# Residual stored to the output early, feed-forward term added there by accumulating transfers from GpSimd

## The reference

```
x = x + attention(mix(x, cond_weights[token]))          # 32 heads, 8 key/value heads, causal, rotary
h = mix(x, cond2_weights[token])
q_in, s_in = quantize(h)        # s_in = max|h| / 448; h / s_in clipped to +-448, rounded to fp8 values
y = (q_in * s_in) @ (fp8(qweight) * w_scale).T + bias
q_out, s_out = quantize_no_rounding(y)                  # s_out = max|y| / 448; y / s_out clipped to +-448
out = x + q_out * s_out
```

## Time and profile before

| | us |
|---|---|
| median of 3 runs (lowest, highest) | 550.52 (549.91, 550.93) |
| the profiled execution | 550.2 |
| span in its profile, first to last instruction | 548.4 |
| TensorE busy | 519.4 (95% of the span) |
| VectorE busy | 353.9 (65%) |
| GpSimd busy | 232.1 (42%) |
| ScalarE busy | 212.3 (39%) |

### The profile page before, as it was taken

One profiled execution on the slowest core, in us unless ns is written; L12 is line 12 of the kernel. 1 busy time (PEld: TensorE's weight loads), 2 busy tenths in 40 slices (PEclk: granted clock), 3 DMA queues, 4 the chain that ended last, 5 costly groups with the idle time before them and its releaser, 6 DMA issues.

```text
span 548.4 us, 8842 instructions
## 1 busy us (share of the span) xinstructions
PE 519.4 (95%) x3244; PEld 414.9 (76%) x3244; DVE 353.9 (65%) x536; ACT 212.3 (39%) x372; POOL 232.1 (42%) x184
## 2 busy tenths in 40 slices
PE   4999999999999999999999999999999999999680
PEld 2987888888888888888888888888888888887420
DVE  5538255666676667666766676667566756675697
ACT  2514214342534263416341634253516251612524
POOL 4426422642664266426632673267326732610002
PEclk9899999999999999999999999999999999999875
DMA  7540500020012011201020202020202000000004
GB/s 250 178 154 0 173 2 1 1 97 1 16 64 96 0 32 44 96 0 52 24 96 0 73 3 96 0 76 2 93 0 76 5 1 0 2 1 0 2 0 153
DMA packets 18046, 26.88 MB, mean 49 GB/s; under 512 B 1995, under 2 KB 6219, under 8 KB 18028
## 3 DMA queue, kind: packets, MB, share of 16 engines
q1 hardware_dynamic: 18028, 26.63, 14.4%
HBM read 24.53 MB, written 2.10 MB: 49 GB/s over the span
## 4 chain that ended last, share of the span: by engine, by line
PE 90%; DVE 7%; issue 1%; DMA 1%; SPq 0%; ACT 0%; DVEq 0%
PE bank L526 27%; PE bank L527 26%; PE bank L528 26%; PE bank L590 3%; PE bank L577 3%; PE bank L518 1%; PE bank L645 1%; DVE f_max L911 1%; PE bank L506 1%; DVE xacc L964 1%; DVE v_all L959 1%; DMA wsc<-in_L_ffn_weight_scale 1%; DVE w L759 1%; DVE q_cos L212 1%; DVE v_all L906 0%
## 5 line engine op out<-in xcount | busy, mean ns | idle before, releaser
L780 DVE TENSOR_TENSOR q_cos<-bank,cst 128x512 f32<-128x512 f32 x80 | 55.3, 691 | 105.1 <-ACT q_swap L396 105.1
L295 POOL TENSOR_TENSOR q_rot<-q_cos,q_swap 128x512 f32<-128x512 f32 x64 | 82.6, 1291 | 89.1 <-DVE q_swap L782 89.1
L526 PE MATMUL bank<-wo_hi,o_hi 128*128 128x512 f32 x256 | 101.6, 397 | 1.2 <-issue 1.2
L526 PE MATMUL bank<-hT_hi,wq_hi 128*128 128x512 f32 x256 | 101.3, 396 | 0.0
L527 PE MATMUL bank<-wo_lo,o_hi 128*128 128x512 f32 x256 | 99.8, 390 | 0.0
L527 PE MATMUL bank<-hT_lo,wq_hi 128*128 128x512 f32 x256 | 99.8, 390 | 0.0
L528 PE MATMUL bank<-wo_hi,o_lo 128*128 128x512 f32 x256 | 99.6, 389 | 0.0
L528 PE MATMUL bank<-hT_hi,wq_lo 128*128 128x512 f32 x256 | 99.6, 389 | 0.0
L395 ACT ACTIVATE q_swap<-bank 64x512 f32<-64x512 f32 x80 | 47.7, 596 | 132.1 <-PE bank L528 132.1
L825 DVE TENSOR_TENSOR xacc<-xacc,bank 128x512 f32<-128x512 f32 x64 | 43.4, 677 | 42.7 <-PE bank L528 42.5
L274 POOL TENSOR_TENSOR wo_lo<-raw_o,wo_hi 128x512 fp32r<-128x512 f32 x32 | 43.7, 1387 | 58.7 <-ACT wo_hi L385 58.7
(11 more groups left out here) (137 smaller groups left out, 721.5 us busy)
## 6 DMA issues: line engine op xcount, KB each, us to landing
raw_q<-in_L_attn_wq SPq DMA_DIRECT2D x8, 1024.0 KB, 5.6
raw_o<-in_L_attn_wo SPq DMA_DIRECT2D x8, 1024.0 KB, 5.2
xacc<-in_x SPq DMA_DIRECT2D x4, 512.0 KB, 8.0
raw_k<-in_L_attn_wk SPq DMA_DIRECT2D x8, 256.0 KB, 2.7
out<-xacc SPq DMA_DIRECT2D x8, 256.0 KB, 2.0
raw_o<-in_L_attn_wv SPq DMA_DIRECT2D x1, 1024.0 KB, 6.8
raw_q<-in_L_attn_wv SPq DMA_DIRECT2D x1, 1024.0 KB, 6.8
q_rot<-in_L_ffn_qweight SPq DMA_DIRECT2D x1, 1024.0 KB
```

The source lines that it names most:

```text
L295: pool.tensor_tensor(dst, q_cos[b][:], q_swap[b][:], ALU.add).then_inc(rope_done, 1)
L526: pe.matmul(dst, l_hi, r_hi, start=(i == 0), stop=False)
L780: dve.tensor_tensor(by_t(q_cos[b][:]), by_t(q_ps[ITEM_BANK[k]][:]), cos_b, ALU.mult).then_inc(rope_cos, 1)
```

## The change

Three things change together. First, SyncE's stores move: each tile of `xacc` is stored to the output as soon as the attention sum is complete (`acc_done`), counted by a new semaphore `dma_plain`, and SyncE's last wait is still for `dma_out`. Second, nothing adds the residual on an engine any more: GpSimd waits for all eight stores and then issues eight transfers that add `f_div(t)` (256 KB each) to what stands in the output, in the order of tiles 7, 0, 6, 1, 5, 2, 4, 3. Third, tiles 4 to 7 are scaled by VectorE alone, from the last down: one instruction multiplies the bank by column 9 and takes the minimum with 448 (`divide_below`), one takes the maximum with -448 and multiplies by column 7 (`scale_above`). Tiles 0 to 3 are multiplied by ScalarE, clipped by VectorE, and multiplied by column 7 by ScalarE again.

```diff
             for t in range(TILES):
-                if t in BY_POOL:
-                    sp.wait_ge(result_pool, BY_POOL.index(t) + 1)
-                else:
-                    sp.wait_ge(result, t + 1 - sum(p < t for p in BY_POOL))
-                sp.dma_start(out_rows[t], xacc[:, t, :]).then_inc(dma_out, 16)
+                sp.wait_ge(acc_done, TPU * 2 * (KV - 1) + t + 1)
+                sp.dma_start(out_rows[t], xacc[:, t, :]).then_inc(dma_plain, 16)
             sp.wait_ge(dma_out, 16 * TILES)
...
-            for i, t in enumerate(BY_POOL):
-                pool.wait_ge(f_back, i + 1)
-                pool.tensor_tensor(xacc[:, t, :], f_div(t), xacc[:, t, :], ALU.add).then_inc(result_pool, 1)
+            pool.wait_ge(dma_plain, 16 * TILES)
+            for i in range(TPU):
+                for ready, t in ((f_scaled, TILES - 1 - i), (f_back, i)):
+                    pool.wait_ge(ready, i + 1)
+                    pool.dma_start(out_rows[t], f_div(t), accum_op=ALU.add).then_inc(dma_out, 16)
...
-            for t in range(TILES):
-                f_divide(t)
-                b = {BY_POOL[0] + 2: BY_POOL[0], BY_POOL[1] + 1: BY_POOL[1]}.get(t)
-                if b is not None:
-
-                    act.wait_ge(f_clip, b + 1)
-                    act.activation(f_div(b), f_div(b), ACT.Copy, scale=col[:, 7:8]).then_inc(f_back, 1)
+            def f_scale_back(t):
+
+                act.wait_ge(f_clip, t + 1)
+                act.activation(f_div(t), f_div(t), ACT.Copy, scale=col[:, 7:8]).then_inc(f_back, 1)
+
+            f_divide(0)
+            f_divide(1)
+            f_scale_back(0)
+            f_divide(2)
+            f_scale_back(1)
+            f_divide(3)
+            f_scale_back(2)
+            f_scale_back(3)
...
-            def add_back(t):
-
-                dve.wait_ge(f_clip, t + 1)
-                dve.scalar_tensor_tensor(out=xacc[:, t, :], in0=f_div(t), scalar=col[:, 7:8], in1=xacc[:, t, :],
-                                         op0=ALU.mult, op1=ALU.add).then_inc(result, 1)
-
-
+            def divide_below(i):
+
+                t = TILES - 1 - i
+                dve.tensor_scalar(f_div(t), bank[t][:], col[:, 9:10], FP8_MAX, ALU.mult, ALU.min).then_inc(f_below, 1)
+
+            def scale_above(i):
+
+                t = TILES - 1 - i
+                dve.wait_ge(f_below, i + 1)
+                dve.tensor_scalar(f_div(t), f_div(t), -FP8_MAX, col[:, 7:8], ALU.max, ALU.mult).then_inc(f_scaled, 1)
+
+            dve.wait_ge(tail_vec, 9)
+            divide_below(0)
             clip(0)
-            clip(1)
-            add_back(0)
-            clip(2)
...
-            add_back(7)
+            scale_above(0)
+            for i in range(1, TPU):
+                divide_below(i)
+                clip(i)
+                scale_above(i)
```

More of the change, by code:

```diff
@@ L40 @@
 V_LATE = 4
-BY_POOL = (1, 3)
 BIAS_ROWS = 33
@@ L140, in build @@
         dma_x = [dma_x] + [sem(f"dma_x{i}") for i in range(1, TILES // 2)]
-        dma_qk, dma_o, dma_out = sem("dma_qk"), sem("dma_o"), sem("dma_out")
+        dma_qk, dma_o, dma_out, dma_plain = sem("dma_qk"), sem("dma_o"), sem("dma_out"), sem("dma_plain")
         const_done, ones_zeroed, warm_done = sem("const_done"), sem("ones_zeroed"), sem("warm_done")
@@ L157, in build @@
         bias_step, bias_done, bias_hi_done = (sem(n) for n in ("bias_step", "bias_done", "bias_hi_done"))
-        f_mm, f_amax, f_kept, f_step, f_div_done, f_clip, f_back, result, result_pool = (
-            sem(n) for n in ("f_mm", "f_amax", "f_kept", "f_step", "f_div_done", "f_clip", "f_back", "result", "result_pool"))
+        f_mm, f_amax, f_kept, f_step, f_div_done, f_clip, f_back, f_below, f_scaled = (
+            sem(n) for n in ("f_mm", "f_amax", "f_kept", "f_step", "f_div_done", "f_clip", "f_back", "f_below", "f_scaled"))
         x_rows = x.rearrange("(j b) c h -> j (b c) h", b=BPT)
@@ L959, in clip @@
                 dve.tensor_scalar(f_div(t), f_div(t), FP8_MAX, -FP8_MAX, ALU.min, ALU.max).then_inc(f_clip, 1)
-            def add_back(t):
-                dve.wait_ge(f_clip, t + 1)
-                dve.scalar_tensor_tensor(out=xacc[:, t, :], in0=f_div(t), scalar=col[:, 7:8], in1=xacc[:, t, :],
-                                         op0=ALU.mult, op1=ALU.add).then_inc(result, 1)
-            clip(0)
-            clip(1)
-            add_back(0)
-            clip(2)
[L972 to L980, removed]
-            add_back(7)
+            def divide_below(i):
[7 more added lines that the diff above has]
+            divide_below(0)
+            clip(0)
+            scale_above(0)
[3 more added lines that the diff above has]
+                scale_above(i)
 _INS = ["x", "itok_B_0_15", "L0_cond_weights", "L0_attn_wq", "L0_attn_wk", "L0_attn_wv", "L0_attn_wo",
```

## The result

The changed kernel takes 555.38 us (median of 4 runs, 554.2 to 556.0) against 550.39 us for the kernel before in the same runs: 1.0083 times, 95% interval 1.0071 to 1.0095, or 5.0 us slower. The direction was as forecast. The size was not: 2.1 us had been forecast, and 5.0 is more than twice that. The time lies just inside the range, by 0.1 us. One execution of 1335.66 us, in the run with all additions on VectorE, is left out of the ratio given there.

What follows compares the result with a forecast made beforehand. VectorE's work, then one transfer's fixed landing, bound the tail. First data at 539.0 plus 10.7 us of transfers, 0.42 landing and 0.4 end gave 550.5, 2.1 above 548.4; 550.52 + 2.1 = 552.6 us, range 547.0 to 555.5.

Steps and rivals of the forecast that it cites:

- Early stores cost nothing: Attention-sum stage: eight 256 KB stores from 481, down by about 515, over 20 us before GpSimd needs them; price zero.
- Last tile ready at 542.1: Tail, VectorE and ScalarE: last scaled tile at 542.1 where the last result came at 545.94, 3.8 us less.
- First data at 539.0: Tail: first accumulation issued at 537.7, its data starting at 538.6 to 539.3, taken as 539.0.
- Issue on GpSimd 1.07 us each: Tail, GpSimd: eight issues one after another, 1.07 us each, 8.6 us in all, from 537.7 to 546.3.
- Transfer 1.34 us each: Tail, DMA engines: each adding transfer takes store plus load time, 1.34 us; eight back to back take 10.7 us.
- The high end of my bound: Tail, adding transfer of one tile: store and load times added, 1.34 us, against a low end of 0.68.
- Landing and end of span 0.82 us: End of tail: 0.42 us from last data to landing, then 0.4 us to the end of the span.
- transfers late and not issues: Tail: transfers end after GpSimd's issues, giving 552.6 us, own range 551.1 to 554.1; chance 0.41.
- the case of issues of 1.59 us: Tail, GpSimd: 1.59 us per issue without hold-up, giving 555.2 us; within the GpSimd-late rival, chance 0.16.
- The gain: Tail rival: issues at most 0.55 us, adding no dearer than a store, giving 546.6 to 547.3 us; chance 0.19.
- the middle case: Tail rival: issues of 0.84 to 1.07 us, transfers at plain rate, giving 548.5 to 551.1 us; chance 0.24.
- The hold-up of GpSimd by VectorE: Tail rival: issuing stands still during VectorE's SBUF-to-SBUF instructions, 2.9 us, giving 554.0 us; GpSimd-late chance 0.16.

Runs made afterwards that it cites:

- the run that issued last: The changed kernel, but GpSimd issues its first adding transfer only when all eight tiles are scaled; 559.90 us, 1.0175 times the kernel before.

## Why the prediction was wrong in size

The forecast tail was 14.4 us (536.12 to 550.5), the measured one is 17.5: 3.1 us missing. By its own steps:

1. *Early stores cost nothing.* Right, both by the changed kernel (down by 512) and by themselves (1.0003).
2. *Last tile ready at 542.1, 6.0 us into the tail.* Measured 6.2 (542.75 less 536.51). A group of three on VectorE was put at 1.34 us and takes 1.39 where nothing disturbs it. Right. That this is worth 3.8 us if the way out were as before is nearly confirmed too: 3.4 by the run with SyncE's plain stores.
3. *First data at 539.0, 2.9 us into the tail.* Wrong by 0.8: measured 3.7 (540.2 less 536.51). I allowed 1.3 us from the ready tile to the data, the middle between SyncE's 0.87 and an issue of 1.07 with 0.54 behind it. GpSimd needs 2.1: 0.6 from the ready tile to the issue, for which the sum had nothing and SyncE shows under 0.1 (537.68 to 537.76 in its run), and 1.5 from the issue to the data.
4. *Issue on GpSimd 1.07 us each, over at 546.3.* Somewhat too dear, and without consequence: eight take 7.3 us where 8.6 was forecast, and they end 9.5 us into the tail and not 10.2. They are not in one row either; with lengths of 1.0 to 2.8 us they overlap. As forecast, the issues were not what ended last.
5. *Transfer 1.34 us each, 10.7 for eight.* The largest miss: 12.7 us (540.2 to 552.9), 1.59 each. The halving itself was right, and slightly overstated: at 205 to 207 GB/s a tile takes 1.27 us. The sum took that rate from the first byte. Adding into HBM starts slower: up to 546 the changed kernel had moved some 0.76 MB in 5.8 us, 130 GB/s, where 206 would have needed 3.7: 2.1 us. The rest took 0.4 us more than at 206, and the forecast rate had 0.5 in hand; that makes the missing 2.0. The high end of my bound, two full-speed streams laid end to end, was taken for an upper end, and it is none: one adding transfer alone shows 2 us of data.
6. *Landing and end of span 0.82 us.* Measured 1.1 (552.9 to 554.0), 0.3 more.

0.8 + 2.0 + 0.3 = 3.1. The step that failed is thus the transfers' term, 1.34 us each from the first byte on, and after it GpSimd's way to the first data. The mechanism named as likeliest, transfers late and not issues, was the right one; it was under-sized by a start that I had no row for. That the time is inside the stated range is luck: the forecast's own range ended at 554.1, and what stretched it to 555.5 was the case of issues of 1.59 us, which did not occur.

The rivals. The gain asked for issues of at most 0.55 us and transfers at the plain rate. The changed kernel has neither, but the plain stores from GpSimd have both (0.54, and 352 to 369 GB/s from 543 to 546), and their 549.25 us is 2 us or more above the gain's 546.6 to 547.3: that case left out the 0.6 us ahead of the issue, the 1.4 to the first data, and the queueing of the last stores. That 549.25 lies inside the middle case's 548.5 to 551.1 is luck, since that case had issues of 0.84 to 1.07 us. The hold-up of GpSimd by VectorE would have given 554.0 and issues of 1.59 us 555.2, the nearest of all to the result, and both for the wrong reason: the eight issues took 7.3 us and not 12.7, and as long with VectorE idle. So the rule of the Trainium skill ("SBUF — State Buffer", section "Who interferes with whom" and the summary) on starved descriptor generation did not show here as a price in time. The other one ("Collectives: The Full Stack", section "The bandwidth ceiling"), half the rate of a copy for a reduction, agrees with 174 to 194 against 385 GB/s for adding within SBUF and 206 against 380 to 389 for adding into HBM; that two reads are the reason no run here shows.

What stays open is why adding into HBM starts slowly. It is not VectorE or the number of issues alone (11.7 us of data remain with two issues and VectorE idle, where 206 GB/s would need 10.2), and not GpSimd still issuing (the run that issued last was at 188 to 203 GB/s from 548 to 550 while GpSimd worked on; a transfer alone was slow after its issue had ended). That it is the time to get the first old values back from HBM would fit, but no run shows it.

## What to carry to other kernels

Work moved from an engine into a transfer is not free because the engine's row disappears: price it in time of all DMA engines, and look for how long they have before the end. An adding transfer takes the data time of two plain ones in steady flow, of three when alone, and comes later from GpSimd than from SyncE; in a tail in which everything becomes ready within 6 us of its start there is nothing to hide it behind, while the early stores, which had 25 us, were indeed free. And when an engine is taken away from a collision, as here GpSimd from VectorE, giving its work to the busy engine can already bring a gain (0.7 us here). Whether the dealt scaling, worth 3.4 us with the cheapest way out, can be kept with the residual added in another way was not tried.

## What the runs showed of the hardware

- An adding transfer of 256 KB from SBUF into HBM, issued by GpSimd, alone: 3.8 us from issue to landing, 0.86 of it the issue's row, about 2 the data. A plain one the same way: 2.3, 0.54 and 0.7. Ahead of each issue 0.5 to 0.6 us pass after the wait is over.
- Steady rates of output: adding into HBM about 206 GB/s (stretches of 195 to 209), adding within SBUF 174 to 194, plain stores from SyncE 380 to 389, plain stores from GpSimd 352 to 369.
- From first to last data 2.10 MB of adding into HBM took 12.7 us (changed kernel), 12.1 (all issued behind the scaling) and 11.7 (two of 1 MB).
- The share of the DMA engines does not tell the rate: it was 1.12 at 143 GB/s and 1.13 at 205.
- TensorE, VectorE and ScalarE have the same work ahead of the tail in all thirteen kernels, and they began it at 535.3 to 537.5. Two of them differ in TensorE's granted clock in the feed-forward stage. Before, and then after, both from 526 to 530:

```profile
526.00:530.00 4.00, 4.00 (x14) 1.28 (x12) 4.00 (x9) 0.00 (x0) 0.00 (x0) 0.88 0.00 0
```
```profile
526.00:530.00 4.00, 4.00 (x9) 1.29 (x9) 4.00 (x8) 0.00 (x0) 0.00 (x0) 0.50 0.00 0
```

  0.50 is the 1.2 GHz level, and 0.88 a stretch that went mostly at 2.4. The changed kernel began that stage 1.4 us sooner and finished it 0.4 us later. Of the kernels with all early stores one began the tail at 536.10 and another at 536.71, so the stores don't fix it. But in the profiles the mean granted clock from 512 to 536 is 0.64 in five of the eight kernels that have them all, and 0.70 to 0.79 in the five kernels that don't; whether they make the low clock commoner is open, and ten executions against 21 leave at most 0.7 us for it. It is why tails, and medians over several runs, are compared here rather than spans.
